# One-chunk adjacency steps, aligned source blocks and one-hots shared by two engines, in a graph attention and expert kernel

## The chip, the cores and the metric

One core of a Trainium2 chip. The metric is the device time of one execution in microseconds, as the median of several runs.

## The reference, cut to what matters

A graph of 3125 nodes with 256 features and 100,000 weighted edges, sorted by target `dst`, goes through a graph attention layer, a feed-forward layer and a layer of 32 experts.

```python
q, k, v = linear(x, wq, bq), linear(x, wk, bk), linear(x, wv, bv)
scores = sum(q[dst] * k[src]) * scale + (edge_weight[:, None] @ we + be)[:, 0]
attn = exp(scores - segment_max(scores, dst)[dst]) / segment_sum(exp(...), dst)[dst]
out = segment_sum(v[src] * attn[:, None], dst)
x = layer_norm(x + out + linear(x, ws, bs)); x = layer_norm(x + ffn(x))
# then: router argmax over 32 experts, expert = relu(relu(x W1 + b1) W2 + b2)
```

## The kernel before, in words

The five engines run programs of their own and meet at semaphores. The work has these stages.

**Ahead of the loop.** ACT, PE and DVE make the queries, keys and values of the 25 tiles of 125 nodes. Meanwhile DVE prepares the edges (98 partitions of 8 chunks of 128 edges). It places *steps*: a step is up to `SUB` = 2 chunks whose targets are looked at through a window of `WIN` = 5 nodes. Counts over all `NS` = 392 step starts (L990, L991, and L1017, L1018 for the last row of each window) give each of 1024 step slots its chunks. SP stores the edge table; POOL gathers it back by slots, 16 indirect DMAs (L598); DVE makes the codes relative to the window (L1026), PE transposes, ACT writes `code_tab` and `nval_tab`. POOL sets the constant rows of `dist_rows` with one memset (L602).

**The adjacency loop** (`turns`, L406: 32 turns of 16 groups, the first and last turn written out with constants, the ones between in a hardware loop with addresses in registers). A group is 2 steps of 2 chunks. The adjacency row of a target over all sources, exp of the edge weight where there is an edge, is built as a product of two matrices of each chunk's 128 edges. For each chunk:
- PE, `distances` (L1349 to L1358): a matmul over 5 rows gives the squared distance of an edge's source, within its block of 125, to each of 128 columns;
- ACT, `columns` (L778 to L786): Relu(exp weight x (1 - distance)), which leaves the weight in one column: `Ys`;
- DVE, `one_hot` (L1053 to L1059): `Xs`, a one-hot over the 125 codes (5 window nodes x 25 source blocks), two chunks at once;
- PE, `product` (L1363 to L1372): Xs^T Ys, the two chunks of a step accumulated in PSUM, in fp32. The two passes of an fp32 matmul are two records, so a group has 8.

DVE, `sums` (L1065 to L1085), then adds a step to the one before it, kept or not by `keep_tab`: `stage[k] = stage[k-1] * keep + product` (L1081). Each sum reads what the last one wrote and waits for its semaphore (`sum_ord`, `sums_ready`). Behind each sum DVE makes one one-hot pair of the group three ahead. Before a group's first sum, DVE waits for the product, for the sum before and, at L1069, for the store of four groups before, since `stage` and `Xs` have `STAGES` = 4 buffers:

```python
dve.wait_ge(prod_done, g + 1)
wait_from(dve, stored[q], 16 * ((BODY // STAGES) * i + j // STAGES))
```

SP, `put` (L515 to L524), stores each group to `adj` in DRAM with one DMA (125 partitions x 2 x 512 B), loads the distance rows once in 8 groups (`load_rows`, L494) and zeroes a part of `xs_dram` once in 8. POOL is idle in the loop, but for the first two gathers of adjacency tiles (`fetch`, L617 to L627), which start as soon as the rows of the first two tiles are stored.

**Attention**, 25 tiles. POOL gathers the tile's adjacency rows (125 x 3200 columns); DVE turns zeros into -1e30 (`exclude`, L1104); PE makes the scores against all keys, which are split in two fp32r parts, by blocks of 512, the last of 128 (L1392, six matmuls each); DVE adds the exclusion and finds the maximum (L1112); ACT exponentiates (L793); DVE multiplies by the adjacency (L1122); PE transposes (L1411) and multiplies with the values (L1404). At its start ACT and DVE split the keys (L801, L1098), and SP builds the expert table `w_dram` (L532).

**Feed-forward and experts** follow; the change leaves them as they are, but for the size of a scratch tensor.

Of the kernel before, what the change touches and what calls it, by code (L numbers as in the profile page):

```python
# [4 lines left out]
F32 = mybir.dt.float32  # L5
# [21 lines left out]
SUB = 2  # L27
# [55 lines left out]
def gnn_moe(nc, x, src, dst, edge_weight, wq, bq, wk, bk, wv, bv, ws, bs, we, be, g1, b1, g2, b2,  # L83
            w_ff1, b_ff1, w_ff2, b_ff2, router_w, router_b, W1, eb1, W2, eb2, out):
    ctx = ExitStack()
    with ctx:
# [16 lines left out]
        xs_dram = nc.dram_tensor("xs_dram", [MT * P, D], F32)  # L103
# [14 lines left out]
        dist_rhs = sb("dist_rhs", [DIST, LO], BF16)  # L118
# [35 lines left out]
        ARENA = 19050  # L154
# [22 lines left out]
        cmp_o = view(4 * P)  # L177
        s_row, o_row, iota_c = view(4 * P), view(4 * P), view(4 * P)
        cmp_s, s_row, o_row, iota_c = (v[:, 0:NS] for v in (cmp_o, s_row, o_row, iota_c))
# [15 lines left out]
        Xs = view(STAGES * GC * TILE).rearrange("p (s k m) -> p s k m", s=STAGES, k=GC)  # L195
# [33 lines left out]
        k_flat = kT[:, :, :, :].rearrange("p k j l -> p (k j l)")  # L229
# [29 lines left out]
        st0 = tables[0:TILE, KH * ROW - 6 * NT:KH * ROW].rearrange("p (t c) -> p t c", c=6)  # L259
        assert 2 * SLOTS * SUB + SLOTS + 7 * NT <= KH * ROW  # L260
# [15 lines left out]
        nmr = tables[0:TILE, KH * ROW - 7 * NT:KH * ROW - 6 * NT]  # L276
# [19 lines left out]
        gath_in = [sem(f"gath_in{b}") for b in range(SBLK)]  # L296
# [33 lines left out]
        xs_v, ys_v = (v.ap().rearrange("(j p) d -> p j d", p=P) for v in (xs_dram, ys_dram))  # L330
# [124 lines left out]
        def _(sp):  # L455
# [30 lines left out]
            for b in range(SBLK):  # L486
                sp.wait_ge(gath_in[b], 16 * SUB)
# [27 lines left out]
            def put(g, j, i):  # L515
# [3 lines left out]
                if j % LOADG == LOADG - 2 and not (isinstance(i, int) and i == TURNS - 1):  # L519
# [3 lines left out]
                sp.dma_start(adj_v[:, bass.ds(g * GROUP, GROUP), :],  # L523
                             stage[0:TILE, j % STAGES, :, :]).then_inc(stored[j % STAGES], 16)  # L524
# [40 lines left out]
        def _(pool):  # L565
# [10 lines left out]
            nc.gpsimd.iota(iota_row[:, :], [[1, P]], base=0, channel_multiplier=0,  # L576
# [5 lines left out]
            nc.gpsimd.memset(kT[:, :, :, TILE:LO], 0.0).then_inc(consts_set, 1)  # L582
# [939 lines left out]
```

## Time and profile before

| | us |
|---|---|
| median of 3 runs (1907.18 to 1913.29) | 1910.41 |
| span of the profiled execution | 1885.6 |
| median less that span | 24.8 |
| DVE, PE, ACT, POOL busy in the span | 1193.9, 1656.9, 965.5, 300.8 |
| granted TensorE clock, mean | 0.917 |

The profiled execution has no time of its own in the results; its span runs from its first to its last instruction, and what a timed run has more lies around it. A busy PE is modelled and is not PE at its peak; register, branch, semaphore and DMA-issuing instructions don't count as busy.

### The profile page before, as it was taken

How to read it: one execution, taken by the hardware profiler on the slowest of the kernel's cores; microseconds unless marked ns; L12 is line 12 of the kernel's file. 1: busy time of each engine (PE TensorE's matmuls, PEld its weight loads, DVE VectorE, ACT ScalarE, POOL GpSimd, SP SyncE). 2: the span in 40 equal slices, each digit the busy share in tenths (PEclk: the TensorE clock that was granted, in tenths of full speed). 3: DMA queues.
4: the chain of work that ended last, by engine and by line, in shares of the span. 5: the costliest groups of instructions: out<-in, count | busy, mean ns of one | idle time of the engine just before them, and what ended most of it. 6: DMA issues, size and time to landing. Idle time of an engine off the chain costs nothing.

```text
span 1885.6 us, 41069 instructions
## 1 busy us (share of the span) xinstructions
PE 1656.9 (88%) x11015; PEld 1378.6 (73%) x11015; DVE 1193.9 (63%) x3327; ACT 965.5 (51%) x2962; POOL 300.8 (16%) x397
## 2 busy tenths in 40 slices
PE   2898999999799999999899999999999789419960
PEld 1796888888688888887688888888888779315640
DVE  3927898988688889898555555555555578701111
ACT  1566888888588888887233333333333345103210
POOL 0022000000000000000111111111110067375435
PEclk9999999999899999999999999999999889656555
DMA  6054333333433333334822222222210100047634
GB/s 159 28 129 115 104 105 104 106 103 105 140 104 104 106 105 103 104 105 112 164 76 77 76 76 76 76 78 75 76 75 37 53 17 0 6 117 214 181 113 121
DMA packets 226999, 180.40 MB, mean 96 GB/s; under 512 B 41884, under 2 KB 218038, under 8 KB 223544
## 3 DMA queue, kind: packets, MB, share of 16 engines
q1 hardware_dynamic: 189327, 112.46, 21.6%
q0 software_dynamic: 21408, 61.20, 9.7%
q10 hardware_dynamic: 16224, 6.27, 1.5%
q8 instruction: 17, 0.28, 0.1%
q14 instruction: 23, 0.19, 0.0%
HBM read 84.94 MB, written 99.11 MB: 98 GB/s over the span
## 4 chain that ended last, share of the span: by engine, by line
PE 78%; DVE 6%; DMA 5%; POOL 4%; issue 3%; SPq 2%; ACT 1%; POOLq 0%; DVEq 0%; ACTq 0%
PE bank L1371 29%; PE bank L1404 15%; PE bank L1392 11%; PE bank L1356 9%; PE bank L1411 3%; PE bank L1486 3%; PE bank L1493 2%; PE bank L1478 2%; PE bank L1444 2%; PE bank L1436 2%; POOL arena L691 2%; POOL xs_dram L669 2%; SPq L458 1%; DMA V<-in_x 1%; DMA arena<-in_x 1%
## 5 line engine op out<-in xcount | busy, mean ns | idle before, releaser
L784 ACT ACTIVATE arena<-bank,tables 128x128 f32<-128x128 f32 x2048 | 585.2, 369 | 144.5 <-PE bank L1356 144.4
L1371 PE MATMUL bank<-arena 128*125 128x128 f32 x4096 | 585.9, 286 | 11.8 <-DVE arena L1055 11.8
L1371 PEld LDWEIGHTS bank<-arena 128*125 128x125 f32 x4096 | 488.4, 188 | 65.1 <-DVE arena L1055 11.9
L1055 DVE TENSOR_TENSOR arena<-iota_row,tables 128x250 f32<-128x250 f32 x1024 | 421.1, 412 | 0.1
L1081 DVE SCALAR_TENSOR_TENSOR arena<-arena,tables,bank 125x128 f32<-125x128 f32 x1023 | 351.9, 344 | 86.5 <-PE bank L1371 37.1
L1404 PE MATMUL bank<-V,arena 125*125 125x256 f32 x1250 | 296.4, 382 | 5.6 <-ACT arena L810 5.6
L810 ACT COPY arena<-bank 125x500 f32<-125x500 f32 (+1 forms) x175 | 90.8, 533 | 379.5 <-PE bank L1411 379.5
L1404 PEld LDWEIGHTS bank<-V,arena 125*125 125x125 f32 x1250 | 223.3, 188 | 38.0 <-ACT arena L810 10.3
L1122 DVE CUSTOM_DVE_ANT_0 arena<-arena 125x3200 f32<-125x3200 f32 x25 | 87.3, 3493 | 222.2 <-ACT arena L793 222.2
L622 POOL COPY gidx<-arow 125x1 uint32 (+1 forms) x25 | 36.4, 1455 | 1182.2 <-DVE wk_sb L1122 856.7
L1356 PE MATMUL bank<-dist_rhs,arena 5*128 5x128 bf16 x2048 | 201.6, 218 | 4.2 <-DVE tables L1039 3.4
L1356 PEld LDWEIGHTS bank<-dist_rhs,arena 5*128 5x128 bf16 x2048 | 113.8, 93 | 66.3 <-issue 4.0
L1392 PE MATMUL bank<-k_hi,q_hi 128*125 128x512 f32 (+1 forms) x350 | 137.7, 393 | 10.3 <-DVE wk_sb L1112 6.9
L1392 PE MATMUL bank<-k_lo,q_hi 128*125 128x512 f32 (+1 forms) x350 | 133.2, 380 | 0.0
L1392 PE MATMUL bank<-k_hi,q_lo 128*125 128x512 f32 (+1 forms) x350 | 133.2, 380 | 0.0
L1112 DVE CUSTOM_DVE_ANT_0 arena<-bank,arena 125x512 f32<-125x512 f32 (+1 forms) x175 | 103.0, 631 | 28.0 <-PE bank L1392 19.1
L793 ACT ACTIVATE arena<-arena,wk_sb 125x512 f32<-125x512 f32 (+1 forms) x175 | 115.8, 679 | 9.6 <-DVE wk_sb L1117 9.6
L1271 DVE TENSOR_SCALAR arena<-bank 128x256 f32<-128x256 f32 x56 | 23.7, 424 | 152.7 <-PE bank L1493 152.7
L1411 PE MATMUL bank<-ident,arena 125*125 125x125 f32 x625 | 94.5, 276 | 2.7 <-issue 2.7
L1411 PEld LDWEIGHTS bank<-ident,arena 125*125 125x125 f32 x625 | 88.7, 190 | 9.4 <-issue 3.1
L1392 PEld LDWEIGHTS bank<-k_hi,q_hi 128*125 128x125 f32 x350 | 65.9, 188 | 30.5 <-DVE wk_sb L1112 13.2
L1478 PE MATMUL bank<-ident,V 128*128 128x128 f32 x112 | 37.2, 434 | 55.1 <-DMA V<-xs_dram 55.1
(219 smaller groups left out, 1665.5 us busy)
## 6 DMA issues: line engine op xcount, KB each, us to landing
adj<-arena SPq DMA_DIRECT2D x512, 125.0 KB
xs_dram<-zeros SPq DMA_DIRECT2D x64, 112.0 KB, 3.2
V<-xs_dram SPq DMA_DIRECT2D x56, 128.0 KB, 2.3
ys_dram<-arena SPq DMA_DIRECT2D x56, 128.0 KB, 1.9
w_dram<-in_L_ffn_W SPq DMA_DIRECT2D x2, 2048.0 KB
V<-in_x SPq DMA_DIRECT2D x5, 625.0 KB
q_dram<-arena ACTq DMA_DIRECT2D x25, 125.0 KB, 2.3
wq_sb<-q_dram SPq DMA_DIRECT2D x25, 125.0 KB, 7.8
```

Source lines behind the costliest of these rows:

```text
L784: ins = nc.scalar.activation(Ys[:, q, k, :], bank[2 + s][:, k * LO:(k + 1) * LO], ACT.Relu, scale=nval_tab[:, bass.ds(i, 1)])
L793: ins = nc.scalar.activation(Z[0:TILE, s, c:c + n], Z[0:TILE, s, c:c + n], ACT.Exp, bias=nmax[:, s:s + 1])
L810: nc.scalar.copy(PT[0:TILE, s, j:j + n, :], bank[4 + g % 2][0:TILE, 0:n * TILE].rearrange("p (n d) -> p n d", n=n)).then_inc(pt_ready, 1)
L1055: ins = V_.tensor_tensor(Xs[:, s, cols, :], iota_row[:, 0:TILE].unsqueeze(1).to_broadcast([P, SUB, TILE]), code_tab[:, bass.ds(g * GC + k ...
L1081: ins = V_.scalar_tensor_tensor(stage[0:TILE, q, k, :], prev, keep_tab[0:TILE, bass.ds(g * GROUP + k, 1)], ps, ALU.mult, ALU.add)
L1112: V_.tensor_tensor_reduce(out=Z[0:TILE, s, c:c + n], in0=bank[b % 4][0:TILE, 0:n], in1=Z[0:TILE, s, c:c + n], scale=1.0, scalar=-BIG, op0= ...
L1122: V_.tensor_tensor_reduce(out=Z[0:TILE, s, :], in0=Z[0:TILE, s, :], in1=A_sb[0:TILE, s, :], scale=1.0, scalar=0.0, op0=ALU.mult, op1=ALU.a ...
L1356: ins = mm(bank[2 + s][:, k * LO:(k + 1) * LO], dist_rows[:, j // LOADG, c:c + CHUNK], dist_rhs[:, :], start=True, stop=True)
L1371: ins = mm(o, Xs[:, j % STAGES, k, :], Ys[:, j % STAGES, k, :], start=(k % SUB == 0), stop=(k % SUB == SUB - 1))
L1392: ins = mm(bank[b % 4][0:TILE, 0:n], q[:, s, k, :], v[:, k, j, :].rearrange("p j l -> p (j l)"), start=(i == 0), stop=(i == len(parts) - 1))
L1404: ins = mm(bank[6 + s][0:TILE, 0:D], PT[0:TILE, s, j, :], V[:, j, :], start=(j == 0), stop=(j == NT - 1))
L1411: ins = tr(bank[4 + g % 2][0:TILE, j * TILE:(j + 1) * TILE], Z[0:TILE, s, (j0 + j) * LO:(j0 + j) * LO + TILE], ident[0:TILE, 0:TILE])
```

## The change

A step is one chunk (`SUB` = 1). The number of steps follows from ceil(100000 / (128 SUB)) + 624, rounded up to whole turns, so 1408 steps in 704 groups of 2, in 44 turns, with 1408 chunk places for 2048. Sources fall into 25 blocks of 128 instead of 125, so the adjacency has its sources in plain order and the scores use 7 blocks of 448 columns (3136). The two chunks of a group have their distance matmuls in two row strips of PE (partitions 0 and 32) and two PSUM banks. POOL makes the one-hots of five groups in eight, one comparison a chunk, from codes that it copies aside; DVE makes those of the groups 1, 4 and 7 of eight. A group is stored with two DMAs, of 112 and of 13 partitions. POOL's `fetch` comes after its part of the loop.

```diff
-SUB = 2
+SUB = 1
-LO = 128
-ROW = NT * LO
+HI, LO = 25, 128
+ROW = HI * LO
+MW = WIN * HI
+EVEN = MW // 16 * 16
+PARTS = 2
+KB = 448
+NCOL = 7 * KB
+STRIP = 32
-ZROWS = MT * P // (2 * TURNS)
+ZROWS = -(-MT * P // (2 * TURNS * 12)) * 12
-SCH = [(c, min(512, ROW - c)) for c in range(0, ROW, 512)]
+SCH = [(c, KB) for c in range(0, NCOL, KB)]
...
+        OWN = (1, 4, 7)
+        def groups_before(j, i, own):
+            mine = [r for r in range(LOADG) if (r in OWN) == own]
+            return i * (BODY // LOADG) * len(mine) + j // LOADG * len(mine) + sum(r < j % LOADG for r in mine)
+        def pool_groups(j, i):
+            return groups_before(j, i, False)
+        def dist_bank(s, k):
+            return bank[2 + s + 4 * k]
...
             def load_rows(n, s):
-                sp.dma_start(dist_rows[2:DIST, s, :], term_rows.ap().rearrange("c i e -> c (i e)")[
-                    :, bass.ds(n * LOADW, LOADW)]).then_inc(rows_in[s], 16)
+                for k in range(GC):
+                    sp.dma_start(dist_rows[k * STRIP + 2:k * STRIP + DIST, s, :].rearrange("c (i e) -> c i e", e=CHUNK),
+                                 term_rows.ap().rearrange("c (i k) e -> c k i e", k=GC)[
+                                     :, k, bass.ds(n * LOADG, LOADG), :]).then_inc(rows_in[s], 16)
...
                 sp.wait_ge(sums_ready, g + 1)
-                sp.dma_start(adj_v[:, bass.ds(g * GROUP, GROUP), :],
-                             stage[0:TILE, j % STAGES, :, :]).then_inc(stored[j % STAGES], 16)
+                for rows_ in (slice(0, EVEN), slice(EVEN, MW)):
+                    sp.dma_start(adj_v[rows_, bass.ds(g * GROUP, GROUP), :],
+                                 stage[rows_, j % STAGES, :, :]).then_inc(stored[j % STAGES], 16)
...
-            nc.gpsimd.memset(dist_rows[0:2, :, :], 1.0).then_inc(ones_set, 1)
+            pool.wait_ge(ws_set, KH + 1)
+            for k in range(GC):
+                if k:
+                    pool.wait_ge(ones_set, k)
+                nc.gpsimd.memset(dist_rows[k * STRIP:k * STRIP + 2, :, :], 1.0).then_inc(ones_set, 1)
...
+            def hold_codes(n, h):
+                nc.gpsimd.tensor_copy(held[:, h, :], code_tab[:, bass.ds(n * HELD, HELD)]).then_inc(codes_held, 1)
+            hold_codes(0, 0)
+            def one_hots(g, j, i):
+                h = j // LOADG
+                if j % LOADG == 0:
+                    pool.wait_ge(codes_held, 2 * i + h + 1)
+                if j % LOADG == 2 and not (isinstance(i, int) and i == TURNS - 1 and h):
+                    wait_from(pool, x_ready, pool_groups(j - 2, i))
+                    hold_codes(2 * i + h + 1, 1 - h)
+                if j % LOADG in OWN:
+                    return
+                wait_from(pool, prod_done, g - STAGES + 1)
+                pool.sem_inc(pool_mark, 1)
+                for k in range(GC):
+                    c = j % LOADG * GC + k
+                    ins = nc.gpsimd.tensor_scalar(Xs[:, j % STAGES, k, :], iota_row[:, 0:MW], held[:, h, c:c + 1], None,
+                                                  ALU.is_equal)
+                ins.then_inc(x_ready, 1)
+            turns(pool, one_hots)
...
-            def one_hot(g, s, k):
...
+            def one_hots(g, q):
+                V_.tensor_tensor(Xs[:, q, :, :], iota_row[:, 0:MW].unsqueeze(1).to_broadcast([P, GC, MW]),
+                                 code_tab[:, bass.ds(g * GC, GC)].unsqueeze(2).to_broadcast([P, GC, MW]),
+                                 ALU.is_equal).then_inc(own_x_ready, 1)
...
                     ins.then_inc(sum_ord if k < GROUP - 1 else sums_ready, 1)
-                    if not (isinstance(i, int) and i == TURNS - 1 and j > BODY - STAGES):
-                        one_hot(g + STAGES - 1, (q - 1) % STAGES, k)
+                last = isinstance(i, int) and i == TURNS - 1 and j > BODY - STAGES
+                if (j + STAGES - 1) % LOADG in OWN and not last:
+                    one_hots(g + STAGES - 1, (q - 1) % STAGES)
...
                 for k in range(GC):
-                    c = ((j % LOADG) * GC + k) * CHUNK
-                    ins = mm(bank[2 + s][:, k * LO:(k + 1) * LO], dist_rows[:, j // LOADG, c:c + CHUNK], dist_rhs[:, :],
+                    rows_ = slice(k * STRIP, k * STRIP + DIST)
+                    ins = mm(dist_bank(s, k)[:, 0:LO], dist_rows[rows_, j // LOADG, c:c + CHUNK], dist_rhs[rows_, :],
                              start=True, stop=True)
...
-                pe.wait_ge(x_ready, g + 1)
+                if j % LOADG in OWN:
+                    pe.wait_ge(own_x_ready, groups_before(j, i, True) + 1)
+                else:
+                    pe.wait_ge(x_ready, pool_groups(j, i) + 1)
+                wait_from(pe, sums_ready, g - STAGES + 1)
+                wait_from(pe, sums_ready, g - STAGES + 1)
```

The arena, the key tensors and the score columns take the new sizes; the step counts are spread over two PSUM banks (784 columns) with a semaphore for the copy, and 11 gathers of the edge table share 6 semaphores.

## Rows read from the trace of the kernel before

**Rows 1.** Busy time by stage, the adjacency loop; us, busy (instructions), clock, DMA share, GB/s.
```profile
157.00:888.00 731.00, 717.55 (x6144) 602.22 (x6144) 642.35 (x2050) 585.21 (x2048) 3.25 (x4) 0.99 0.37 106
```
**Rows 2.** Chain of waits in the loop: start, us, what.
```profile
165.28 0.32 PE bank L1356 x4
165.60 1.07 PE bank L1371 x8
```
**Rows 3.** Timeline of DVE in the loop: start, us, engine, line, instruction.
```profile
302.42 0.41 DVE L1055 TENSOR_TENSOR arena<-iota_row,tables 128x250 f32<-128x250 f32 x1
302.75 0.34 DVE L1081 SCALAR_TENSOR_TENSOR arena<-arena,tables,bank 125x128 f32<-125x128 f32 x1
```
**Rows 4.** Chain of waits around 481 us; DVEq is DVE's sequencer.
```profile
480.31 0.02 DVEq L1075
480.33 0.05 issue
480.38 0.07 DVEq L1081
480.46 0.05 issue
...
481.65 17.52 DMA adj<-arena
```
**Rows 5.** Timeline of DVE, end of the last turn.
```profile
885.54 2.48 DVE L1081 SCALAR_TENSOR_TENSOR arena<-arena,tables,bank 125x128 f32<-125x128 f32 x6
```
**Rows 6.** Timeline of DVE in attention; in brackets the idle time before.
```profile
945.85 0.43 DVE L1139 BATCH_NORM_STATS2 wv_sb<-x 125x6 f32<-125x256 f32 x1 [0.15 <-DVE x L1138]
```
**Rows 7.** Timeline of SP in the loop.
```profile
303.27 1.49 SPq L523 DMA_DIRECT2D adj<-arena  x2
305.00 0.28 SPq L495 DMA_DIRECT2D arena<-term_rows  x1
```
**Rows 8.** SP's line 523, 200 to 400 us: ns min/median/max.
```profile
L523 SPq DMA_DIRECT2D adj<-arena x144: 263/264/276, 200.0 to 399.2; - x144
```
**Rows 9.** POOL's groups by form: busy us, mean ns, idle before.
```profile
L598 POOL DMA_INDIRECT arena<-edge_tab,cidx x16 | 15.5, 969 | 111.8 <-DMA edge_tab<-arena 107.2 <-issue 4.6
...
L647 POOL TENSOR_SCALAR wk_sb<-wk_sb 125x1 f32<-125x1 f32 x50 | 15.4, 308 | 3.7 <-DVE wk_sb L1185 2.9 <-DVE wk_sb L1207 0.8
...
L589 POOL TENSOR_TENSOR ws_sb<-ws_sb,ident 128x128 f32<-128x128 f32 x2 | 0.9, 454 | 14.1 <-DMA bq_col<-in_L_gnn_bq 14.1
```
**Rows 10.** DVE's groups by form, ahead of the loop.
```profile
L991 DVE TENSOR_REDUCE cnt<-arena 128x1 f32<-128x392 f32 x8 | 4.5, 561 | 0.3
L990 DVE TENSOR_SCALAR arena<-arena,step_col 128x392 f32<-128x392 f32 x8 | 3.4, 426 | 0.3
...
L979 DVE TENSOR_REDUCE guards<-arena 98x1 f32<-98x196 f32 x2 | 0.7, 357 | 0.1
```
**Rows 11.** Timeline, POOL and DVE at 145 us, POOL at 911 us.
```profile
145.49 6.91 POOL L602 MEMSET arena<- 2x8192 bf16 x1
146.95 5.61 DVE L1026 TENSOR_SCALAR arena<-arena,wneg 128x256 f32<-128x256 f32 x1 [2.27 <-DMA arena<-edge_tab,cidx]
...
911.56 1.61 POOL L622 COPY gidx<-arow 125x1 uint32<-125x1 uint32 x1 [428.45 <-DVE wk_sb L1122]
```
**Rows 12.** DMA issues: median us from issue to landing.
```profile
arena<-adj,gidx POOLq DMA_INDIRECT x25, 15.8
```
**Rows 13.** Timeline of DVE, start of attention.
```profile
896.41 1.82 DVE L1104 TENSOR_SCALAR arena<-arena 125x3200 f32<-125x3200 f32 x1
```
**Rows 14.** Chain of waits in one attention tile.
```profile
979.96 8.99 PE bank L1392 x42
```
**Rows 15.** Busy time by stage, early in the loop (columns as in rows 1).
```profile
160.00:163.50 3.50, 3.50 (x19) 3.08 (x18) 1.20 (x4) 2.09 (x8) 0.00 (x0) 0.50 0.02 4
```
**Rows 16.** Chain of waits, early in the loop.
```profile
159.54 2.00 PE bank L1371 x8
```
**Rows 17.** DVE's line 1164 (inputs x, mean, g_row): ns min/median/max.
```profile
L1164 DVE SCALAR_TENSOR_TENSOR x<-x,mean,g_row x25: 473/476/946, 1486.6 to 1595.5; 125x256 f32<-125x256 f32 x15, 125x256 f32 x10
```

More of the change, by code:

```diff
@@ L153, in gnn_moe @@
         x1 = sb("x1", [TILE, NT, D])
-        ARENA = 19050
+        ARENA = 19260
         arena = sb("arena", [P, ARENA])
@@ L176, in gnn_moe @@
         assert SBLK * SUB * TABW <= edges_only
[L177 to L179 removed]
+        cmp_o = view(NS)
+        s_row, o_row, iota_c = view(NS), view(NS), view(NS)
+        cmp_s = cmp_o
         diag_flat = view(SBLK * P)
@@ L295, in gnn_moe @@
             "code_set", "idx_set", "rel_set", "tabT_done", "tab_set", "keep_set"))
-        gath_in = [sem(f"gath_in{b}") for b in range(SBLK)]
+        s_copied, codes_held, own_x_ready = sem("s_copied"), sem("codes_held"), sem("own_x_ready")
+        gath_in = [sem(f"gath_in{b}") for b in range(-(-SBLK // 2))]
+        gathered = [16 * min(2, SBLK - 2 * b) for b in range(-(-SBLK // 2))]
         last_set, last_stored, last_in, arow_set = (sem(n) for n in ("last_set", "last_stored", "last_in", "arow_set"))
@@ L329, in gnn_moe @@
         x_t = x.rearrange("(t p) d -> p t d", p=TILE)
-        xs_v, ys_v = (v.ap().rearrange("(j p) d -> p j d", p=P) for v in (xs_dram, ys_dram))
+        xs_v, ys_v = (v.ap()[0:MT * P, :].rearrange("(j p) d -> p j d", p=P) for v in (xs_dram, ys_dram))
         out_t = out.rearrange("(t p) d -> p t d", p=TILE)
@@ L609, in _ @@
             pool.wait_ge(q_stored[1], 16 * (NT // 2))
+            pool.wait_ge(ones_set, GC)
+            pool.wait_ge(tab_set, SBLK)
+            pool.wait_ge(terms_stored, 16 * SUB * SBLK)
+            def hold_codes(n, h):
[12 more added lines that the diff above has]
+                pool.sem_inc(pool_mark, 1)
+                for k in range(GC):
+                    c = j % LOADG * GC + k
[3 more added lines that the diff above has]
+            turns(pool, one_hots)
             last_group = (2 * TILE // WIN + NS - 2) // GROUP
@@ L783, in columns @@
                     i = g * GC + k
-                    ins = nc.scalar.activation(Ys[:, q, k, :], bank[2 + s][:, k * LO:(k + 1) * LO], ACT.Relu,
+                    ins = nc.scalar.activation(Ys[:, q, k, :], dist_bank(s, k)[:, 0:LO], ACT.Relu,
                                                scale=nval_tab[:, bass.ds(i, 1)])
@@ L970, in _ @@
             dve.wait_ge(rows_bc, 1)
-            od(V_.tensor_copy(s_row, bank[0][:, 0:NS]))
+            od(V_.tensor_copy(s_row[:, 0:512], bank[0][:, 0:512]))
+            od(V_.tensor_copy(s_row[:, 512:NS], bank[1][:, 0:NS - 512]))
+            dve.sem_inc(s_copied, 1)
             od(V_.memset(s_row[:, 0:1], 0.0))
@@ L1317, in spread @@
                 pe.wait_ge(diag_set, 1)
-                mm(bank[0][:, 0:NS], ones[0:PP, :], s_diag, start=True, stop=True).then_inc(rows_bc, 1)
+                mm(bank[0][:, 0:512], ones[0:PP, :], s_diag[:, 0:512], start=True, stop=True)
+                mm(bank[1][:, 0:NS - 512], ones[0:PP, :], s_diag[:, 512:NS], start=True, stop=True).then_inc(rows_bc, 1)
                 pe.wait_ge(diag_set, 2)
+                pe.wait_ge(s_copied, 1)
                 mm(bank[1][:, 0:4 * PP], ones[0:PP, :], e_diag, start=True, stop=True).then_inc(rows_bc, 1)
```

116 lines of the change are left out of this document (56 added, 60 removed).

## The prediction

> **What bounds the kernel now.** Busy time by stage comes first. The adjacency loop fills 157 to 888 us, 731 us of the 1885.6 us span, with PE busy 717.6 us, DVE 642.3, ACT 585.2, POOL idle, DMA at 0.37 [rows 1]. The chain of waits is then all PE: four distance matmuls in 0.32 us and eight product records in 1.07, 1.39 us for a group of four chunks, 512 times [rows 2]. DVE is close behind: a sum starts 0.33 us after the one-hot ahead of it [rows 3], and each one-hot covers whatever the next sum has to wait for. Once the loop loses 17.5 us to one adjacency store, while the first two adjacency gathers use the DMA engines (last line of [rows 4]).
>
> **The loop, engine by engine.** Chunks (2 a group, 704 groups) fall from 2048 to 1408, steps rise from 1024 to 1408. PE: half a group, 0.16 + 0.54 = 0.70 us; strips in two row groups can only lower it. ACT: 585.2/2048 x 2 = 0.57 us [rows 1]. Both drop out of the bound.
>
> DVE keeps two sums a group and loses most of the one-hots, and the cover goes with them. The sums form one chain: each reads the row the last one wrote and waits for its semaphore. How far apart do they start? The last turn, written out with constant addresses, has six sums in 2.48 us [rows 5], (2.48 - 0.35)/5 = 0.43 each, 0.86 a group. In the loop a register step for the keep_tab address stands between the wait and the sum: after L1075's wait (0.02) come 0.05, L1081's register step 0.07 and 0.05, so 0.19 us at a group's first sum [rows 4], and 0.12 plus 0.04 to wake, 0.16, at its second. A dependent DVE instruction with a register address elsewhere waits 0.15 [rows 6]. So a group is (0.35 + 0.16) + (0.35 + 0.04 + 0.19) = 1.09 us. Today the one-hot hides all of this. The three own one-hots in eight groups fit into the boundary gap (0.25 after a sum's start, 0.33 long) and cost 0.02 more.
>
> Here a rule speaks against me. The Trainium skill (VectorE: DVE Perf Modes, "The DRAIN you can't avoid") says that the pipeline flush comes anyway and a semaphore between two DVE instructions adds nothing. The last turn's spacing of 0.43 for 0.35 us sums nearly agrees; the gap of 0.15 does not, because of the register step. By the rule alone a group would be about 0.87; that is the first rival.
>
> SP issues two stores a group instead of one, and two row loads in eight groups instead of one. A store's issue takes 0.26 us [rows 8]; the second of two stores ends at 303.27 + 1.49 = 304.76, so it began at 304.49, and the row load behind it at 305.00: 0.51 us apart with nothing to wait for [rows 7]. In eight groups: eight first stores at 0.51, eight second ones between 0.31 (no register step) and 0.51, two row loads at 0.51, one zero fill at about 0.5: 8.1 to 9.7 us, 1.01 to 1.21 a group. SP so becomes as tight as DVE. DVE feels it, since a sum waits for the store of four groups before. A store over 112 partitions and one over 13 should land earlier than one over 125, and 4 x 1.1 us is enough time for it.
>
> POOL: ten comparisons in eight groups. Nearest rows: a one-input instruction on one column 0.31, a two-input one on 128 columns 0.45 [rows 9]; ten cost 3.1 to 4.5 us plus waits, of 9. It becomes the bound only from 0.9 us each. Nothing.
>
> I take 1.13 us a group, between DVE's 1.09 and the middle of SP's range above it, as the two alternate: 42 turns x 16 x 1.13 = 759, the two written-out turns 32 x 0.95 = 30, start and end 4: **793 us against 731, +62**. The stall of 17.5 us is in the 731 and goes: its gathers now come after the loop.
>
> **Ahead of the loop** DVE is on the chain. A compare and a reduction over 392 steps (0.43 + 0.56 + 0.07) are repeated 8 + 5 times; over 784 the reduction grows by 0.41 (its slope: 0.20 for 196 columns) and the compare by up to 0.41, I take 0.2, so 1.67: 11 x 1.67 - 8 x 1.06 + 5 x 0.61 = +13 [rows 10]. Wider copies and diagonals: +3.5, an estimate. 16 gathers of (15.5 + 4.6)/16 = 1.26 us become 11: -6.3 [rows 9]. DVE's last small addition now takes 5.61 us under a POOL memset of 6.91 [rows 11]; the memset shrinks to two of a quarter: -3 (0 to -5). Sum **+7**.
>
> **At the loop's end** POOL fetches the first adjacency tile after its last one-hots, some 4 us before the last sum, instead of mid-loop. A gather lands after 15.8 us, so 13 us or more behind the last sum, where DVE now needs it at 896.4, 8.4 us behind [rows 12, 13]. The w_dram copies start at the same moment. **+9** (5 to 20).
>
> **Attention**: 25 tiles with 42 score matmuls in 8.99 us [rows 14]. 3136 columns for 3200 save 0.18 us a tile, -4.5; evening out the narrow block may save up to 0.45 (-11); if the whole time were the wide blocks' it would cost +5. I take **-6**.
>
> The remaining edits (bank split of the row spread, a longer xs_dram, 84-row zero fills, held codes copied on POOL, doubled waits) hide behind the chains above.
>
> Sum: +62 + 7 + 9 - 6 = +72. The profiled execution has a span of 1885.6 us; the runs have a median of 1910.4, so 24.8 us lie around it, and I leave those: 1910 + 72 = **1982 us**. The change pays only below (731 - 10 - 34)/672 = 1.02 us a group.
>
> **Rivals.**
> 1. *The register steps overlap* (the rule above). For it: 0.43 spacing in the written-out turn [rows 5]. Against: the waits stand in front of the register step in the chain [rows 4], and the 0.15 gap [rows 6]. SP must also run near its low end: 8 x (0.51 + 0.31) + 2 x 0.31 + 0.35 = 7.5 us, 0.94 a group. Then 672 x 0.94 + 34 = 666, -65 + 10: **1855 us**. Chance 0.24.
> 2. *TensorE's clock falls.* Its matmuls fill 0.70 of 1.13 us, where now they are back to back. At the 1.2 GHz level eight records take 2.00 us rather than 1.07 and the granted clock is 0.50 [rows 15, 16]; a group would then be 1.0 + 0.3 = 1.3 us and PE the bound. But at that pace it rose within a few us, so half the time: 1.215 a group, +119 + 10: **2039 us**; it decides as soon as the low level makes PE slower than 1.13. Chance 0.07.
> 3. *POOL and DVE exclude each other.* The trace has it: a 0.35 us-sized addition that took 5.61 beside POOL's memset, a one-column POOL copy of 1.61 beside a DVE pass [rows 11]; but also a two-SBUF-input DVE instruction beside POOL work with median 476 ns and only a maximum of 946 [rows 17]. If each own one-hot waited out a comparison (0.45 x 3/8 = 0.17 a group) the sum is 2100; for half of it **2039 us**. Chance 0.06. The Trainium skill (SBUF — State Buffer, "SBUF: two separate sides") calls it an exclusive lock on a shared port pair, taken by DVE instructions with two SBUF inputs. The long rows agree; the median of 476 shows how rarely it bites.
> 4. *Near even*: 1.00 to 1.04 a group, the gaps a little shorter than I read. Chance 0.08, 0.05 of it within the bound.
>
> **The numbers.** My own case, group 1.08 to 1.22 us, has 0.55 and reaches from 1949 to 2043 us. With the rivals the range is 1845 to 2055. A measurement of this kernel can tell about 0.3%, 6 us, from no change. Faster: 0.24 + 0.03 = 0.27; same: 0.05; slower: 0.55 + 0.07 + 0.06 = 0.68.
>
> **What the next profile would show.** Right: in the loop PE busy near 65% and DVE under 80%, sums 0.50 and 0.6 us apart with idle time in front put down to DVE itself or to the adjacency store, SP's issues without a pause; POOL busy under half; the chain made of DVE and SP pieces; 704 groups in about 793 us; no 17 us stall; the first exclusion pass 13 us or more after the last sum; the first distance matmul at about 164 us. Wrong: sums 0.43 apart in the loop (rival 1), the granted clock under 0.9 there (2), one-hots on DVE over 0.6 us (3). If SP's second store is issued within 0.3 us and sums still stand 1.1 us a group, the chain on DVE alone was the cause; if the sums wait for stores, SP was.

## The result and the profile after

The changed kernel takes 2147.5 us (median of 4 runs, 2127.3 to 2150.2) against 1911.9 (median of 4, 1907.2 to 1916.6) for the kernel before: ratio 1.1219, 95% interval 1.1156 to 1.1282. The forecast was 1982 with a range up to 2055: slower was right, the size was not, 236 us for a forecast of 72. Runs of one kernel differ by up to 2%, the longer ones at a lower granted clock (e3: 1945.0 us at 0.940, 1976.9 at 0.912); the ratios below rest on runs without this disturbance, and as the profiled executions of e3 and e9 are disturbed ones, only periods and single rows are used of them.

The stages come first, as in [rows 1]: ahead of the loop, the adjacency loop, the first attention tiles, the attention, the rest. Columns: stretch, us, busy us and instructions of PE, PEld, DVE, ACT, POOL, granted clock, DMA share, GB/s.

```profile
0.00:164.00 164.00, 107.88 (x684) 94.80 (x684) 90.50 (x207) 73.01 (x225) 18.13 (x31) 0.96 0.38 96
164.00:1138.00 974.00, 967.67 (x4243) 725.06 (x4244) 600.12 (x1682) 447.67 (x1417) 538.48 (x972) 0.50 0.41 104
1138.00:1220.00 82.00, 65.48 (x310) 57.18 (x309) 38.28 (x85) 20.97 (x40) 8.38 (x6) 0.90 0.59 142
1220.00:1737.00 517.00, 497.95 (x2575) 437.78 (x2575) 269.49 (x606) 174.58 (x332) 55.86 (x40) 1.00 0.19 69
1737.00:2147.00 410.00, 270.44 (x1282) 201.16 (x1280) 156.22 (x390) 103.35 (x315) 208.13 (x312) 0.65 0.32 95
```

The loop's row answers to [rows 1] and holds the main part of the story: the granted clock is 0.50, the 1.2 GHz level, for all of 974 us, where it was 0.99. PE does two thirds of the chunks and is busy for longer, 967.7 us for 717.6. The page's chain of waits gives PE nearly everything:

```profile
PE 79%; issue 6%; DVE 5%; DMA 4%; SPq 2%; POOL 2%; ACT 1%; DVEq 0%; POOLq 0%; ACTq 0%
PE bank L1440 37%; PE bank L1471 12%; PE bank L1459 9%; PE bank L1420 7%; PE bank L1553 3%; PE bank L1478 3%; PE bank L1560 2%; PE bank L1511 2%; PE bank L1503 2%; PE bank L1545 2%; POOL arena L752 1%; SPq L483 1%; DMA V<-in_x 1%; DMA arena<-adj,gidx 1%; DMA arena<-in_x 1%
```

L1440 makes the products, L1420 the distances. One group in the timeline at 500 us (start, us, engine, line, instruction, idle time before and its releaser), and under it PEld's rows:

```profile
499.96 1.22 PE L1440 MATMUL bank<-arena 128*125 128x128 f32 x4
501.11 0.29 PE L1420 MATMUL bank<-dist_rhs,arena 5*128 5x128 bf16 x2
501.32 1.22 PE L1440 MATMUL bank<-arena 128*125 128x128 f32 x4
501.33 0.35 DVE L1141 SCALAR_TENSOR_TENSOR arena<-arena,tables,bank 125x128 f32<-125x128 f32 x1 [0.52 <-PE bank L1440]
501.83 0.35 DVE L1141 SCALAR_TENSOR_TENSOR arena<-arena,tables,bank 125x128 f32<-125x128 f32 x1 [0.15 <-DVE arena L1141]
```

```profile
499.96 0.92 PEld L1440 LDWEIGHTS bank<-arena 128*125 128x125 f32 x4
501.10 0.10 PEld L1420 LDWEIGHTS bank<-dist_rhs,arena 5*128 5x128 bf16 x2 [0.23 <-issue]
501.32 0.92 PEld L1440 LDWEIGHTS bank<-arena 128*125 128x125 f32 x4
```

Products start 501.32 - 499.96 = 1.36 us apart. By the starts of its first and last sum (169.4 and 1129.3 us) the loop ran 959.9 us for 703.5 groups, 1.364 each, so this group is typical. PE waits for no engine. DVE waits 0.52 us for PE at the first sum and 0.15 for itself at the second: that 0.15 is the gap of [rows 6], in which the forecast placed the register step (e5 below prices it). Once in each group the weight loads pause for 0.23 us with nothing to wait for ("issue"). The page's groups of instructions (busy, mean ns, idle before and releaser) say the same of the other engines:

```profile
L1141 DVE SCALAR_TENSOR_TENSOR arena<-arena,tables,bank 125x128 f32<-125x128 f32 x1407 | 489.0, 348 | 370.0 <-PE bank L1440 246.2
L667 POOL TENSOR_SCALAR arena<-iota_row,arena 128x125 f32<-128x125 f32 x880 | 520.8, 604 | 423.2 <-PE bank L1440 418.3
L845 ACT ACTIVATE arena<-bank,tables 128x128 f32<-128x128 f32 x1408 | 440.9, 364 | 519.7 <-PE bank L1420 519.0
```

How did it come to the low level? Both kernels enter the loop at 0.50, after PE has waited on DVE. In the kernel before, PE was then busy for all of [rows 15], and the clock was 1.00 from 163.5 us on (columns as in the stages):

```profile
163.50:170.00 6.50, 6.50 (x57) 5.38 (x57) 5.55 (x18) 4.75 (x17) 0.00 (x0) 1.00 0.27 77
```

In the changed kernel it stays at 0.50:

```profile
166.00:168.00 2.00, 0.51 (x5) 0.25 (x3) 0.80 (x3) 1.65 (x7) 1.95 (x4) 0.50 0.05 12
168.00:170.00 2.00, 2.00 (x9) 1.66 (x10) 0.64 (x2) 0.65 (x3) 2.00 (x4) 0.50 0.00 0
170.00:175.00 5.00, 5.00 (x24) 3.62 (x23) 2.80 (x9) 2.08 (x7) 3.05 (x6) 0.50 0.34 84
175.00:185.00 10.00, 10.00 (x45) 7.59 (x45) 6.17 (x18) 4.82 (x16) 6.32 (x11) 0.50 0.43 109
```

The PE column is full from 168 us, and still the granted clock stays at 0.50. PE's busy time alone would not have shown the trouble, only the clock column does. Beside it, weight loads fill 7.59 of 10 us here and filled 3.08 of 3.50 in [rows 15]; most of what is missing is the pause of 0.23 us in each group. It is a difference between the two, and e7 below shows that it is no rule.

At the loop's other end stand the rows that answer to [rows 5] and [rows 13]:

```profile
1127.15 2.46 DVE L1141 SCALAR_TENSOR_TENSOR arena<-arena,tables,bank 125x128 f32<-125x128 f32 x6 [0.31 <-PE bank L1440]
1130.73 7.10 DVE L1158 TENSOR_TENSOR k_lo<-kT,k_hi 128x896 fp32r<-128x896 f32 x7 [1.13 <-ACT k_hi L861]
1145.02 1.80 DVE L1165 TENSOR_SCALAR arena<-arena 125x3136 f32<-125x3136 f32 x1 [7.19 <-DMA arena<-adj,gidx]
```

The first exclusion pass starts 1145.02 - 1129.61 = 15.4 us behind the last sum, where it was 8.4, and now waits 7.19 us for the fetch of the adjacency tile. The 17.5 us stall inside the loop is gone.

### The profile page after: what moved, and what is told of

The parts are those of the page before. It is cut to its first block, busy times and chain, and to the rows that moved or that the text cites. A ratio compares the mean times of both kernels' runs of the same rounds, so it can differ in the third digit from the quotient of the medians.

```text
span 2147.2 us, 43497 instructions
## 1 busy us (share of the span) xinstructions
PE 1909.4 (89%) x9089; PEld 1516.0 (71%) x9089; DVE 1154.6 (54%) x2968; ACT 819.6 (38%) x2328; POOL 829.0 (39%) x1361
## 4 chain that ended last, share of the span: by engine, by line
PE 79%; issue 6%; DVE 5%; DMA 4%; SPq 2%; POOL 2%; ACT 1%; DVEq 0%; POOLq 0%; ACTq 0%
PE bank L1440 37%; PE bank L1471 12%; PE bank L1459 9%; PE bank L1420 7%; PE bank L1553 3%; PE bank L1478 3%; PE bank L1560 2%; PE bank L1511 2%; PE bank L1503 2%; PE bank L1545 2%; POOL arena L752 1%; SPq L483 1%; DMA V<-in_x 1%; DMA arena<-adj,gidx 1%; DMA arena<-in_x 1%
## 5 line engine op out<-in xcount | busy, mean ns | idle before, releaser
L1440 PE MATMUL bank<-arena 128*125 128x128 f32 x2816 | 855.7, 457 | 0.5 <-POOL arena L667 0.5
L1440 PEld LDWEIGHTS bank<-arena 128*125 128x125 f32 x2816 | 647.0, 320 | 82.5 <-POOL arena L667 0.7
L1141 DVE SCALAR_TENSOR_TENSOR arena<-arena,tables,bank 125x128 f32<-125x128 f32 x1407 | 489.0, 348 | 370.0 <-PE bank L1440 246.2
L667 POOL TENSOR_SCALAR arena<-iota_row,arena 128x125 f32<-128x125 f32 x880 | 520.8, 604 | 423.2 <-PE bank L1440 418.3
L845 ACT ACTIVATE arena<-bank,tables 128x128 f32<-128x128 f32 x1408 | 440.9, 364 | 519.7 <-PE bank L1420 519.0
L1420 PE MATMUL bank<-dist_rhs,arena 5*128 5x128 bf16 x1408 | 202.1, 283 | 3.8 <-DVE tables L1102 2.8
L1420 PEld LDWEIGHTS bank<-dist_rhs,arena 5*128 5x128 bf16 x1408 | 72.7, 99 | 163.9 <-issue 133.8
L1459 PE MATMUL bank<-k_hi,q_hi 128*125 128x448 f32 x350 | 138.0, 394 | 30.0 <-DVE wk_sb L1173 26.8
L1459 PE MATMUL bank<-k_lo,q_hi 128*125 128x448 f32 x350 | 130.9, 374 | 0.0
L1459 PE MATMUL bank<-k_hi,q_lo 128*125 128x448 f32 x350 | 130.7, 374 | 0.0
L1117 DVE TENSOR_TENSOR arena<-iota_row,tables 128x250 f32<-128x250 f32 x264 | 123.3, 467 | 0.1
L854 ACT ACTIVATE arena<-arena,wk_sb 125x448 f32<-125x448 f32 x175 | 114.4, 671 | 20.0 <-DVE wk_sb L1178 20.0
```

The lines of the kernel that those rows point to most:

```text
L667: ins = nc.gpsimd.tensor_scalar(Xs[:, j % STAGES, k, :], iota_row[:, 0:MW], held[:, h, c:c + 1], None, ALU.is_equal)
L845: ins = nc.scalar.activation(Ys[:, q, k, :], dist_bank(s, k)[:, 0:LO], ACT.Relu, scale=nval_tab[:, bass.ds(i, 1)])
L854: ins = nc.scalar.activation(Z[0:TILE, s, c:c + n], Z[0:TILE, s, c:c + n], ACT.Exp, bias=nmax[:, s:s + 1])
L1117: V_.tensor_tensor(Xs[:, q, :, :], iota_row[:, 0:MW].unsqueeze(1).to_broadcast([P, GC, MW]), code_tab[:, bass.ds(g * GC, GC)].unsqueeze(2) ...
L1141: ins = V_.scalar_tensor_tensor(stage[0:MW, q, k, :], prev, keep_tab[0:MW, bass.ds(g * GROUP + k, 1)], ps, ALU.mult, ALU.add)
L1420: ins = mm(dist_bank(s, k)[:, 0:LO], dist_rows[rows_, j // LOADG, c:c + CHUNK], dist_rhs[rows_, :], start=True, stop=True)
```

## The experiments

All start from the changed kernel unless another is named. The theory after the first look: three limits lie one above the other, PE at the low clock (1.36 us a group), SP's issues, DVE's chain of sums, and each hides the next. The rivals: it is PE's work as such, or POOL, and the clock only follows. "Period" is the time from the start of the first sum to that of the last over 703.5 pairs of chunks; "clock" is the granted clock of 300 to 700 us; the medians are over all runs of a kernel, and each ratio is to the kernel before on the same chip. Code is cut to the lines that matter. The times alone are too coarse for small effects: behind the start of the last attention tile the profiled execution of the changed kernel takes 445 us and that of e6 421 us for the same work. So the periods carry the argument.

| kernel | period us | clock | median us | before | ratio (95%) |
|---|---|---|---|---|---|
| changed | 1.364 | 0.50 | 2147.5 | 1911.9 | 1.122 (1.116-1.128) |
| e1 two dummies | 1.292* | 0.95 | 2095.1 | 1904.8 | 1.100 (1.089-1.111) |
| e10 one dummy | 1.292 | 0.81 | 2079.9 | 1878.5 | 1.107, one run |
| e2 pair store | 1.364 | 0.50 | 2141.5 | 1904.8 | 1.124 (1.116-1.132) |
| e3 dummies, pair store | 1.113 | 1.00 | 1960.9 | 1904.8 | 1.021, one run |
| e6 e3, no POOL one-hots | 1.107* | 1.00 | 1957.1 | 1881.7 | 1.042 (1.028-1.056) |
| e11 pair store, held flags | 1.364 | 0.50 | 2132.4 | 1878.5 | 1.135, one run |
| e5 e3 and held flags | 0.924 | 1.00 | 1834.4 | 1881.7 | 0.977 (0.968-0.986) |
| e4 groups of four | 1.083 | 0.78 | 1939.9 | 1904.8 | 1.018 (1.010-1.026) |
| e7 four, held flags | 0.897 | 0.94 | 1809.2 | 1881.7 | 0.963 (0.954-0.973) |
| e8 e7 and dummies | 0.900 | 1.00 | 1815.6 | 1881.7 | 0.967 (0.950-0.983) |
| e9 e7, wide score blocks | 0.893 | 0.94 | 1792.8 | 1878.5 | 0.955 (0.945-0.965) |

\* Less one wait at the loop's end, which belongs to neither limit. There a sum waits for an adjacency store while the first adjacency gathers run, as in the 17.5 us stall of the kernel before. With the wait the periods are 1.315 and 1.127. (Waits of under 4 us at the same place in e4, e7 and e8 are left in.) The first sums behind it, in e1 and in e6:

```profile
1095.45 0.73 DVE L1141 SCALAR_TENSOR_TENSOR arena<-arena,tables,bank 125x128 f32<-125x128 f32 x2 [15.64 <-DMA adj<-arena]
958.81 0.73 DVE L1145 SCALAR_TENSOR_TENSOR arena<-arena,tables,bank 125x128 f32<-125x128 f32 x2 [13.77 <-DMA adj<-arena]
```

### e1 and e10: raise the clock alone

Each group gets two bf16 matmuls of 256 columns (e10: one) on constant data into the unused half of its product bank, ahead of its products. They add work to the very engine that the chain names.

```
+ warm = ones[:, :].bitcast(BF16)
+ for _ in range(2):          # e10: range(1)
+     mm(product_bank(j)[:, 256:512], warm[:, 0:P], warm[:, 0:256], start=True, stop=True)
  for k in range(GC):
```

> The changed kernel with two dummy matmuls more in each group (bf16, 128 rows, 256 columns, into a part of the product bank that nobody reads). Theory A, PE's clock alone made the loop long: the dummies keep PE busier, the granted clock in the loop goes back towards 1.0, and the group falls from the measured 1.365 us to the next limit; SP's issues add up to 8 x 1.075 + 2 x 0.57 + 0.6 = 10.3 us in eight groups, 1.29 a group, so some 2090 us. Theory B, the clock is only low because something else is slow: the same 1.365 us and about 2147 us, or more. If the dummies don't lift the clock, they cost 2 x 0.21 us in each of 704 groups: about 2450 us.

> The changed kernel with one dummy matmul a group instead of two. If what lifts the clock is how much PE has to do, one dummy does it less often: a granted clock in the loop between 0.50 and the 0.95 that two gave, and a time between 2095 and 2147 us, or up to 2220 if it stays at 0.50 and the dummy is paid for (0.1 us x 704 at least).

Busy time of 300 to 700 us in e1, and of 400 to 500 us in e10:

```profile
300.00:700.00 400.00, 307.01 (x2463) 234.59 (x2461) 253.06 (x732) 193.04 (x617) 234.97 (x424) 0.95 0.43 108
```

```profile
400.00:500.00 100.00, 79.14 (x540) 59.83 (x541) 63.06 (x185) 48.50 (x156) 59.24 (x107) 0.81 0.43 108
```

More work on the engine that ends last made the kernel faster: PE's busy share fell from 100% to 77%. One dummy is enough for most of it, and both kernels have the same period, 1.292: PE is no longer the limit. So the low clock was worth 1.364 - 1.292 = 0.072 us a group, 51 us, and no more, because the next limit stands right above. e10 came out under the bounds that I gave it; 1.107 of its own before, though, is e1's 1.100 within e1's interval, and the two periods agree.

What the next limit is, e1's waits of DVE between 400 and 600 us show (total us, times, longest), and SP's timeline:

```profile
DVE arena L1141 <- DMA adj<-arena: 30.6, 46, 1.1
DVE arena L1141 <- DVE arena L1141: 22.6, 128, 0.3
DVE arena L1141 <- PE bank L1443: 12.8, 38, 0.6
```

```profile
500.66 1.89 SPq L552 DMA_DIRECT2D adj<-arena  x4
503.12 0.33 SPq L545 DMA_DIRECT2D xs_dram<-zeros  x1
503.75 6.21 SPq L552 DMA_DIRECT2D adj<-arena  x12
510.23 0.71 SPq L522 DMA_DIRECT2D arena<-term_rows  x2
```

Twelve stores are issued in 6.21 us without a pause: (6.21 - 0.32)/11 = 0.536 us from one to the next, 1.07 for a group's two. With the row loads, the zero fill and the loop's branch between them, eight groups take 10.3 us, 1.29 each, which is the period. Of e1's chain of waits between 400 and 600 us, SP's store line L552 alone is 35%, the product matmuls of PE 1.4%.

### e2 and e3: halve SP's stores, without and with the clock

The stage buffers become a ring of eight, and SP issues its two stores once in two groups, each over both groups.

```
+ if j % 2 == 0:
+     return
+ q = j % RING          # RING = 8
  sp.wait_ge(sums_ready, g + 1)
  for rows_ in (slice(0, EVEN), slice(EVEN, MW)):
-     sp.dma_start(adj_v[rows_, bass.ds(g * GROUP, GROUP), :], stage[rows_, j % STAGES, :, :]) ...
+     sp.dma_start(adj_v[rows_, bass.ds((g - 1) * GROUP, 2 * GROUP), :], stage[rows_, q - 1:q + 1, :, :] ...) ...
```

> The changed kernel, but two groups are stored at once (ring of 8 stage buffers, two DMAs for two groups). SP's issues fall to about half. Theory A (PE at 1.2 GHz is the bound): nothing changes, 1.365 us a group, 2147 us within 15. Theory C (SP's queue is the bound and PE only looks busy): the group falls to about 1.1 us, 1975 us.

> Both of the above. If A holds and SP is the second limit, the group falls to the chain of sums on DVE, 0.51 + 0.60 = 1.11 us, with idle time of 0.15 and 0.24 us in front of the sums: loop about 790 us, time about 1970 us. If the register steps don't count (the rival of the prediction), 0.9 us a group and about 1830 us. If the clock stays low, about 2450 us.

e2 alone changes nothing: the period is 1.364, the clock 0.50. Together with the dummies (e3) the same edit takes the period from 1.292 to 1.113, (1.292 - 1.113) x 704 = 126 us. That is what "one limit above the other" means: SP's stores cost nothing in the changed kernel as it stands, and 126 us once the clock is up. e3's DVE timeline shows what stands between the sums now:

```profile
502.14 0.35 DVE L1148 SCALAR_TENSOR_TENSOR arena<-arena,tables,bank 125x128 f32<-125x128 f32 x1
502.64 0.35 DVE L1148 SCALAR_TENSOR_TENSOR arena<-arena,tables,bank 125x128 f32<-125x128 f32 x1 [0.15 <-DVE arena L1148]
503.22 0.35 DVE L1148 SCALAR_TENSOR_TENSOR arena<-arena,tables,bank 125x128 f32<-125x128 f32 x1 [0.23 <-PE bank L1450]
503.72 0.35 DVE L1148 SCALAR_TENSOR_TENSOR arena<-arena,tables,bank 125x128 f32<-125x128 f32 x1 [0.15 <-DVE arena L1148]
```

Sums stand 0.50 and 0.58 us apart, 1.08 a group. The forecast had 0.51 and 0.58. But the gap of 0.23 at a group's first sum is put down to PE's product, not to DVE's own register step, and of e3's chain of waits between 400 and 600 us 18.5% are PE's (dummies and products), most of the rest DVE's.

### e5 and e11: take the register step away

At the start of each eight groups the next 16 keep flags are copied to one of two small tiles, and the sums read them there, at constant addresses.

```
+ V_.tensor_copy(kept[:, h, :], keep_tab[:, bass.ds(n * KEPT, KEPT)]).then_inc(keeps_held, 1)
...
- keep_tab[0:MW, bass.ds(g * GROUP + k, 1)]
+ kept[0:MW, h, j % LOADG * GROUP + k:j % LOADG * GROUP + k + 1]
```

> Dummy matmuls, pair stores, and the keep flags of eight groups copied by DVE once into a tile that the sums read at constant addresses, so that no register step stands between a sum's wait and the sum. If the register steps were the third limit (1.11 us a group in the run with dummies and pair stores), the chain of sums falls to 0.38 + 0.49 = 0.87 us and the next limit is PE with its dummies or POOL (5 x 1.18 us and its waits in eight groups, 0.9): 0.9 to 1.0 us a group, about 1850 to 1890 us. If the gap of 0.15 has another cause, it stays at 1.11 us and about 1960 us.

> Pair stores and held keep flags without dummies: both later limits are gone, only PE's clock is left as it was. Theory A: PE stays at 1.2 GHz with 1.365 us a group and the time at about 2140 us. Rival: with the sums earlier PE waits less, its clock rises, and the group falls towards 0.9 us, 1830 us.

DVE's timeline of e5, and its busy time of 300 to 700 us:

```profile
502.60 0.41 DVE L1125 TENSOR_TENSOR arena<-iota_row,tables 128x250 f32<-128x250 f32 x1
502.93 2.39 DVE L1159 SCALAR_TENSOR_TENSOR arena<-arena,bank 125x128 f32<-125x128 f32 x6
505.24 0.43 DVE L1125 TENSOR_TENSOR arena<-iota_row,tables 128x250 f32<-128x250 f32 x1
```

```profile
300.00:700.00 400.00, 400.00 (x3475) 313.74 (x3474) 349.73 (x1086) 270.94 (x868) 329.72 (x597) 1.00 0.62 152
```

Six sums in 2.39 us: (2.39 - 0.35)/5 = 0.41 us apart, closer than the 0.43 of [rows 5]. The period falls from 1.113 to 0.924, 134 us, and the kernel takes 2.3% less (1.4 to 3.2%) than the one before; the time of 1834 us is under the 1850 to 1890 expected, on a chip whose kernel before takes 1882 instead of 1905. Here the Trainium skill (VectorE: DVE Perf Modes, "The DRAIN you can't avoid") says that semaphores add nothing between DVE instructions, and the trace agrees: with all the waits still there, sums of 0.35 us start as little as 0.38 us apart. What costs is the register step behind a wait, and these runs measure it: in the median of 300 to 700 us the second sum of a group starts 0.49 us behind the first in e3 and 0.38 in e5, so the step costs 0.11 us a time, less than the 0.15 us of idle time that the rows show before a sum. e11, the same edit without the dummies, stays at 1.364: the low clock hides this limit too. PE is busy for all 400 us in e5, but at full clock and with the dummies in it; e5's chain of waits between 400 and 600 us, by line, has no PE at all:

```profile
by line: DVE arena L1159 60.4%; issue 26.7%; DVE arena L1125 6.2%; DVEq L1143 2.0%; DVE arena L1134 1.9%; DVEq L1153 1.9%; DVEq L427 0.8%; DVEq L434 0.3%
```

### e6: does POOL hold DVE up?

On top of e3 DVE makes all one-hots, and POOL none.

```
- OWN = (1, 4, 7)
+ OWN = tuple(range(8))
```

POOL's first adjacency gathers, which came after its one-hots, now start 24 groups before the loop's end; that brings the wait which the table leaves out of e6's period.

> Dummies and pair stores, but POOL makes no one-hots and no copies of codes in the loop: DVE makes one pair behind every group's last sum. Theory: they fit into the gap that the chain of sums leaves anyway, so the loop stays near 1.11 us a group (1.11 to 1.17) and the time near 1960 to 2000 us; handing them to POOL bought next to nothing. Rival: DVE pays for each (0.33 us for 5 more of 8 groups, 0.2 us a group): 1.32 us a group, 2105 us.

The groups of DVE and POOL between 300 and 700 us, first of e3, then of e6:

```profile
L672 POOL TENSOR_SCALAR arena<-iota_row,arena 128x125 f32<-128x125 f32 x447 | 275.6, 631 | 118.4 <-PE bank L1450 116.2
...
L1122 DVE TENSOR_TENSOR arena<-iota_row,tables 128x250 f32<-128x250 f32 x134 | 63.7, 475 | 0.0
```

```profile
L1119 DVE TENSOR_TENSOR arena<-iota_row,tables 128x250 f32<-128x250 f32 x360 | 148.6, 413 | 0.0
```

A DVE one-hot takes 475 ns beside POOL and 413 without it, so they do disturb each other, by 62 ns x 3/8 = 0.02 us a group. Laid side by side, single instructions show how: a one-hot of e3 that starts 0.06 to 0.12 us into a POOL comparison of 0.60 us ends 0.03 us behind its end, after 0.52 to 0.57 us; one that starts 0.56 us into it takes its 0.41; and a comparison that starts during a one-hot takes about 0.78 to 0.80 us. So neither waits out the whole of the other, as rival 3 had assumed. The period is nearly the same, 1.107 against 1.113, and with the wait at the loop's end and what follows it the first exclusion pass starts at 970.4 us in e6 and 973.5 in e3: moving five one-hots in eight to POOL bought nothing while the register step stood in the sums, since the one-hots then fill gaps that DVE has anyway. Rival 3 has its direction and about a seventh of its price (0.02 for 0.17 us a group). The ratios, 1.042 and 1.021, differ by more than this; the trace of e3's one run behind 1.021 is not among the profiles, so what makes that difference stays open.

### e4, e7, e8: groups of four

Four chunks a group and 352 groups: one wait of each kind for twice the work, half the stores. The other two take e4 and hold the keep flags as in e5, e8 with dummies in an unused half of a distance bank.

```
- GROUP = 2
+ GROUP = 4
...
- return bank[2 + s + 4 * k]
+ return bank[2 + s + 4 * (k % 2)][:, k // 2 * LO:(k // 2 + 1) * LO]
```

> The changed kernel with groups of four one-chunk steps instead of two (352 groups, still 1408 chunks; PE gets four chunks between two waits, as in the kernel before). Theory A with the cause that short batches leave PE with idle time between them: at the low clock four chunks took 2.53 us in the kernel before and the clock rose from there, so it rises here too, and the loop is then bounded by four sums, 3 x 0.51 + 0.60 = 2.13 us a group: 750 us, time about 1940 us. If the clock stays low, 2.53 us a group or more: 890 us, time about 2070 us.

> Groups of four one-chunk steps and held keep flags. Chain of sums 3 x 0.38 + 0.49 = 1.63 us a group, with DVE's own one-hots of 0.67 us in three of eight groups 1.75; PE at the high clock 1.39. If the clock holds: 352 x 1.75 = 616 us, time about 1800 us. If the clock goes up and down as in the run with groups of four (0.78), PE needs 1.39 to 2.53 us a group: 2.0 us on average, about 1890 us.

> The same with two dummy matmuls of 256 bf16 columns in each group, to keep the clock up. At the high clock PE needs 1.39 + 0.25 = 1.64 us, still under the chain's 1.75: about 1800 us with the granted clock near 1.0 in the loop. If the dummies don't matter for the clock: as the run without them, plus up to 0.25 us a group (90 us).

Stretches of e4, then one of e7 and one of e8 (columns as in the stages):

```profile
200.00:300.00 100.00, 84.45 (x565) 68.64 (x564) 72.97 (x203) 53.68 (x188) 72.91 (x124) 0.73 0.51 130
...
500.00:600.00 100.00, 76.24 (x547) 62.54 (x544) 72.43 (x200) 51.94 (x182) 68.32 (x119) 0.79 0.50 128
```

```profile
300.00:700.00 400.00, 312.70 (x2693) 254.12 (x2692) 357.60 (x1010) 257.21 (x900) 354.93 (x590) 0.94 0.62 157
```

```profile
300.00:700.00 400.00, 342.00 (x3136) 263.68 (x3136) 357.43 (x1007) 254.87 (x895) 346.89 (x588) 1.00 0.62 157
```

With groups of four the clock needs no dummies: it goes up and down (0.73 to 0.79) in e4 and stands at 0.94 in e7, with PE busy for only 78% of the time and weight loads for 64%. e8 brings it to 1.00 and the period stays, 0.900 against 0.897, so PE is not the limit. DVE and POOL are both busy for 89%; e7's chain of waits between 400 and 600 us is DVE's, 72% of it the sums alone. e4 still has the register step, and its period is 1.083, its time the 1940 us expected. It also keeps the two row strips of the distances, so the strips are not what holds the clock down.

### e9: the score blocks wide again

```
- SCH = [(c, KB) for c in range(0, NCOL, KB)]
+ SCH = [(c, min(512, NCOL - c)) for c in range(0, NCOL, 512)]
```

> The groups of four with held keep flags, and the score blocks of the kernel before: six of 512 columns and a last one of 64, instead of seven of 448. Theory: the equal blocks made a tile 0.23 us longer (23.3 against 23.1 us), because DVE's pass over a block is what PE waits for at the end of a tile and a narrow last block frees the banks sooner; so the tile falls to 23.0 us and the time by 5 to 12 us against the run without this edit, to about 1800 us, 0.955 of the kernel before. Rival: the tile's length has to do with the plain column order; then no change.

The group of the first score matmuls (busy, mean ns, idle before), in the changed kernel and in e9 (e7, which differs from e9 in this edit alone, has 138.2 us with 38.2 idle before, 28.8 of it for DVE):

```profile
L1459 PE MATMUL bank<-k_hi,q_hi 128*125 128x448 f32 x350 | 138.0, 394 | 30.0 <-DVE wk_sb L1173 26.8
```

```profile
L1471 PE MATMUL bank<-k_hi,q_hi 128*125 128x512 f32 (+1 forms) x350 | 138.1, 395 | 19.8 <-DVE wk_sb L1185 13.7
```

The matmuls take the same time either way; what differs is how long PE waits for DVE's pass over the block ahead. An attention tile takes 23.35 us in the changed kernel and in e7, 23.03 in e9 and 23.08 before (starts of the one wide DVE instruction that each tile has). So seven even blocks cost 0.27 us a tile over the kernel before, and 0.32 over six blocks of 512 and a narrow one, 8 us in 25 tiles, as expected. The intervals of e7 and e9 overlap, so the gain is read from the tiles and not from the times. e9 has the lowest median of this study: 1792.8 us, 0.955 (0.945 to 0.965) of the kernel before.

## Why the prediction was right or wrong

**Where the 165 us of the miss lie.** In the loop, by the two profiles. From the first distance matmul (165.7 us) to the end of the last sum (1129.6) the loop takes 964 us, +233 against 731; forecast was +62.

The 24.8 us that the forecast left "around" the span were read wrongly. In every run with both on record the time is 1.7 us above its core's span. The profiled execution before, 1885.6 us, was a short one, some 23 us under the median. The forecast of +72 doesn't rest on it, but the difference of the spans, 261.6 us, is 26 more than the 235.6 of the medians, and no record shows in which stage of the timed runs those us lay.

**TensorE's clock: the rival that decided.** Rival 2 had its mechanism, its sign and the price of a full fall (1.3 us a group; measured 1.364) and a chance of 0.07; the sign named for it, a granted clock under 0.9 in the loop, is what the profile shows. Two steps failed. In the sum, "PE: half a group, 0.16 + 0.54 = 0.70 us" took the full clock for granted and let PE "drop out of the bound"; it took 1.36 and was the bound. In the rival, the step is "at that pace it rose within a few us, so half the time". It was taken from [rows 15], where PE works on four chunks for each wait; the changed loop has two, and the stretch in which the clock rose said nothing of it. In e1, e10 and e4, which give PE more work for each wait, useful or not, the clock is 0.95, 0.81 and 0.78. Why the level is held in one loop and not in the other stays open, and so does whether it would have held at 1.00 if the loop had been entered there. At the low level four chunks took 2.00 + 0.54 = 2.54 us before ([rows 16], and 0.54 for the four distance matmuls behind them in the same chain), 0.64 a chunk, and now two take 1.36, 0.68 a chunk.

**SP: a term mis-sized.** Forecast for eight groups: 8.1 to 9.7 us, and the middle of it was taken. Measured in e1: 10.3. The low end let the second store go without a register step, at 0.31; it has one (SP's line L552 shows as many register steps as stores) and costs 0.54 like the first. The high end priced every store at 0.51; with issues of 0.31 to 0.32 us for the 0.26 of [rows 8] they stand 0.536 apart, 0.4 us more in eight groups, and the row loads, the zero fill and the branch took the other 0.2. Without the clock's fall the kernel would then still have been e1's, 2095, outside the range: (1.292 - 1.13) x 704 = 114 of the 165 us are missing on SP's account alone. The period of 1.13 was met only where SP has slack and the clock is up, in e3 with 1.113, and there in part by luck, since PE stands in e3's chain where the forecast had DVE alone. The run of e3 behind the ratio 1.021 takes 1945.0 us, 40 more than the kernel before, for +72 forecast.

**DVE's chain: right, and hidden.** 1.09 forecast, 1.08 between the sums of e3, with the gap of 0.15 where it was placed at the second sum. The first rival, that register steps overlap, is refuted by e3 against e5: without them the group is 0.19 us shorter. In the changed kernel itself this chain limits nothing. The point of break-even, 1.02 us, agrees: e5 at 0.92 is faster than the kernel before, e3 at 1.11 and e4 at 1.08 are not.

**POOL.** Its comparison takes 0.604 us, outside the 0.31 to 0.45 of [rows 9]. It changed nothing at 1.36 a group and may be close to the limit in e7 (89% busy).

**The edges.** Ahead of the loop +8.6 us (165.7 for 157.1) against +7. At its end +7.0 against +9, by the mechanism named. Attention -6 forecast; from the first exclusion pass to the last it takes 557.4 us for 547.8, +10, of which 0.27 a tile throughout and 4 in the first two tiles: the sign was wrong. It rested on columns, which cost nothing here, and not on the pass of DVE that each block waits for; the bound given for it, +5, was nearer. The 17.5 us stall went, as said, but e1 and e6 show that one of 14 to 16 us can come back at the loop's end when the gathers meet the last stores. Sum: +233 + 9 + 7 + 10 = 259 of the 261.6 between the two spans (2147.2 and 1885.6); the stages behind the attention have the rest.

## What to carry to other kernels

Limits stack. Here three stood within 0.25 us of each other, 1.36, 1.29 and 1.11, and removing the second (e2), or the second and the third (e11), below the first changed nothing; in the order from the top each paid, 51, 126 and 134 us. Before work is taken off an engine, ask what stands behind it in each group and which waits the work that is taken away was hiding.

If a change cuts TensorE's work for each wait, read the granted clock of the loop first and do not trust a busy share near 100% at 0.50: a dummy matmul is a cheap test (here e1 and e10). And price a DMA or a chained DVE instruction in a loop with its register steps: a store of 0.32 us took 0.54 here, a sum 0.11 more than at a constant address, and holding the operand at a constant address is a small edit.

## What was not expected of the hardware

- Work added to the bound engine made the kernel faster: one matmul of 0.32 us a group (e10's mean) lifted the granted clock from 0.50 to 0.81, two to 0.95. With four chunks for each wait and no dummy it was 0.78 (e4) and 0.94 (e7). What exactly the chip counts isn't settled by these runs.
- The clock can stay at 0.50 for 974 us in a loop whose PE column is full.
- A store of 112 or of 13 partitions is issued in 0.32 or 0.31 us, one of 125 in 0.26: the two parts together cost 2.4 times the issue time of the whole, and the small part hardly less than the large one.
- A POOL comparison of 128x125 against a column takes 602 ns in the median (changed kernel, 300 to 700 us); in e7 the median is 601, but single ones take up to 1120 and lift the mean to 646.
